# One written order of steps per engine for the first attention with the routing and shared expert beside it, without the identity matmuls before its scores

## The reference, cut to what matters

```
x = x + gated_recurrence_and_ffn(ln(x))           # layer 0, "front"
x = x + attention(ln(x), ctx, ctx)                # 16 heads of 8, rotary, key mask: the FIRST attention
x = x + mixture(ln(x))                            # shared expert + 8 routed experts, top 2, width 256
x = x + attention_of_24_picked_rows(ln(x))
x = x + attention(ln(x), ctx, ctx)                # the last attention
x = x + capacity_mixture(ln(x))                   # 8 experts of width 512

mixture(x):   probs = sigmoid(x @ router.T + bias); scores, idx = top_k(probs, 2); scores /= sum(scores)
              shared = (silu(x @ sg.T) * (x @ su.T)) @ sd.T
              routed = sum over the 2 experts e of a token: score_e * ((silu(x @ gate[e]) * (x @ up[e])) @ down[e])
```

## Time and profile before

| what | value |
|---|---|
| times of three runs | 775.45, 776.41 (median), 781.89 us |
| the profiled execution's own time | 780.67 us |
| its span, first to last instruction | 778.9 us (1.8 us around it) |
| mean granted PE clock | 0.878 of full speed |
| busy, share of the span | PE 77%, DVE 56%, PEld 56%, ACT 38%, POOL 30% |

### The profile page before, as it was taken

How to read it: one execution, slowest core, us unless ns; L and a number is a source line. 1 busy time by engine, 2 the same in 40 slices (tenths; PEclk the granted TensorE clock), 3 DMA queues, 4 the chain that set the end, 5 groups by cost and what they waited for, 6 DMA issues and landing times.

```text
span 778.9 us, 15307 instructions
## 1 busy us (share of the span) xinstructions
PE 601.5 (77%) x4751; PEld 432.5 (56%) x4751; DVE 438.5 (56%) x1165; ACT 296.2 (38%) x679; POOL 232.9 (30%) x324
## 2 busy tenths in 40 slices
PE   4699996898778849898716699846799987555992
PEld 2444453665555639798504488623466764534992
DVE  4889787566554554356334566355455642568443
ACT  2585320455334314343202277511145453101661
POOL 6735333001004545243621111022100001353452
PEclk9899998899996989999866899976799997657997
DMA  9955987543200083432100000108543500003014
GB/s 286 323 93 155 274 216 221 130 115 84 66 4 21 30 313 96 122 107 67 47 24 1 0 2 1 50 14 239 131 114 84 127 2 1 0 32 105 25 35 129
DMA packets 87492, 75.71 MB, mean 97 GB/s; under 512 B 10456, under 2 KB 80752, under 8 KB 84512
## 3 DMA queue, kind: packets, MB, share of 16 engines
q1 hardware_dynamic: 82544, 66.80, 31.7%
q0 software_dynamic: 3296, 6.79, 2.9%
q10 hardware_dynamic: 1584, 1.26, 0.5%
HBM read 41.59 MB, written 32.98 MB: 96 GB/s over the span
## 4 chain that ended last, share of the span: by engine, by line
PE 44%; DVE 20%; issue 11%; DMA 7%; POOL 6%; ACT 3%; SPq 3%; another core or an unknown queue 2%; DVEq 2%; POOLq 0%; ACTq 0%
PE ps L2220 5%; PE ps L2104 4%; PE ps L1782 3%; PE ps L1746 3%; PE ps L2088 2%; PE ps L2070 2%; SPq L426 2%; POOL xs_scr L779 2%; PE ps L2323 2%; PE ps L2232 2%; DMA q_scr<-parts 2%; PE ps L1930 2%; PE ps L2066 2%; PE ps L2083 2%
## 5 line engine op out<-in xcount | busy, mean ns | idle before, releaser
L1363 DVE TENSOR_REDUCE negm<-ps 128x4 f32<-128x512 f32 x128 | 85.1, 689 | 63.0 <-PE ps L2070 60.6
L955 ACT ACTIVATE wa<-ps 128x1024 f32<-128x1024 f32 x64 | 65.6, 1025 | 83.0 <-PE ps L2088 80.8
L2220 PE MATMUL ps<-nT,f 128*128 128x128 f32 x368 | 52.3, 287 | 11.3 <-DVE wb L1571 8.4
L2220 PEld LDWEIGHTS ps<-nT,f 128*128 128x128 f32 x368 | 47.1, 200 | 13.7 <-DVE wb L1571 10.0
L2104 PE MATMUL ps<-wa,f 128*32 128x128 f32 x1024 | 42.9, 294 | 2.9 <-ACT wa L955 1.9
L1854 PE MATMUL ps<-identb 128*128 128x512 bf16 x108 | 38.6, 418 | 4.8 <-issue 2.1
L2070 PE MATMUL ps<-stack 75*128 75x128 bf16 x384 | 40.6, 232 | 0.0
L2070 PEld LDWEIGHTS ps<-stack 75*128 75x128 bf16 x384 | 32.4, 105 | 14.6 <-issue 4.8
L711 POOL DMA_INDIRECT x_scr<-y_tok,selT x32 | 31.5, 985 | 28.0 <-ACT stack L1064 18.8
L2088 PE MATMUL ps<-stack 75*128 75x128 bf16 x384 | 35.5, 231 | 2.2 <-DMA stack<-mT 1.5
L784 POOL DMA_INDIRECT y_scr<-f,stack x23 | 25.8, 1121 | 31.5 <-DVE f L1721 21.1
(11 more groups left out here) (391 smaller groups left out, 1508.8 us busy)
## 6 DMA issues: line engine op xcount, KB each, us to landing
k_scr<-parts SPq DMA_DIRECT2D x48, 192.0 KB, 3.0
q_scr<-parts SPq DMA_DIRECT2D x48, 192.0 KB, 3.5
stack<-k_scr SPq DMA_DIRECT2D x12, 600.0 KB, 7.0
stack<-q_scr SPq DMA_DIRECT2D x12, 600.0 KB, 5.3
w_w<-in_w SPq DMA_DIRECT2D x2, 2048.0 KB
x_scr<-sel SPq DMA_DIRECT2D x2, 1472.0 KB, 10.3
x_scr<-stack SPq DMA_DIRECT2D x10, 256.0 KB, 4.9
wb<-q_scr SPq DMA_DIRECT2D x4, 600.0 KB, 5.0
```

Source lines behind the costliest of these rows:

```text
L955: link.release(act.activation(wa[:, u % 2, :], BF[u % 2], ACT.Exp, scale=SCALE), hWA.filled, hWA.at(stage, n * 4 + u), hB.freed)
L1363: v.tensor_reduce(negm[:, g4 * 4:g4 * 4 + 4, j], A[u % 2].rearrange("p (h k) -> p h k", h=4), AX.X, ALU.max, negate=True).then_inc(hA.free ...
L2220: last = mm(A[x % 2][:, c * S:(c + 1) * S], gu_of[x % NGU][:, c * S:(c + 1) * S], nT[:, k % 2, q * S:(q + 1) * S], start=True, stop=True)
```

## The change

The hooks go. Each engine gets one list (`WOVEN`) with every part of the eight steps and every mixture step in one order, "part unit . step" or "kind . block" (x is DVE's maxima, e ACT's exponentials, c POOL's copies, fa and fb the two sets of eight scatters of the first half). The last attention keeps its table, now `STEP`.

```diff
-    for op, u in STEP[0]: ... for s in extra(eng, n, op, u): mixture_step(s[:-2], int(s[-1]))
+    for s in WOVEN[eng]:  attention part, or mixture_step(s[:-2], int(s[-1]))

+        T_TURN = {s: k for k, s in enumerate(s for s in WOVEN["PE"] if s[0] in "MXo" and of_attention(s))}

         def mix_bank(step):
-            return U if step in ("tr.2", "ro.2", "bk.3", "ro.3", "cu.1") else T
+            return dict(T=T, U=U, Z=A[1])[bank_name(step)]
+        def bank_name(step):
+            return "Z" if step in ("po.2", "bk.2", "tr.2", "ro.2") else "U" if step in ("bk.3", "ro.3", "cu.1") else "T"

                 def maxima(n, u):
                     j, g4 = u // 4, u % 4
+                    if a == 0 and u == 0 and n > 0:
+                        v.wait_ge(mp_ready, n)
                     v.wait_ge(hA.filled, hA.at(stage, n * 8 + u))

+                    elif name == "Z":
+                        pe.wait_ge(hA.freed, hA.at("moe0", 1))

                 elif kind == "so":
+                    if n == 1:
+                        pe.wait_ge(dve_front, after("lg.2"))

-                    if a == 0 and True:
+                    if a == 0 and False:
                         keep_warm(bank, 1)

+            def first_rows(part):                       # POOL, fa.0 and fb.0
+                g.wait_ge(zero0_stored, 32)
+                g.wait_ge(dve_front, after("ps.0"))
+                for b in range(part * HB // 2, (part + 1) * HB // 2):
+                    scatter(b, 0)
```

More of the change, by code:

```diff
@@ L1438, in gu_copy @@
                  .then_inc(gu_ready, 1)
-            def closing(part):
-                for s in CLOSE["DVE"][part].split():
-                    mixture_step(s[:-2], int(s[-1]))
             def mixture_step(kind, n):
@@ L1985, in ring_T @@
                 T_next[0] = k + 1
-            def closing(part):
-                for s in CLOSE["PE"][part].split():
-                    mixture_step(s[:-2], int(s[-1]))
             def mixture_step(kind, n):
```

212 lines of the change are left out of this document (125 added, 87 removed), and 17 rows, old and new, of tables (BESIDE, CLOSE, STEP).

## The result

The changed kernel takes 776.33 us (median of 20 runs), the kernel before, timed beside it on the same chips, 781.82 us (20 runs): a ratio of 0.9928, 95% interval 0.9905 to 0.995. It is 5.5 us faster, 0.7%. The forecast said 24.4 us. Some executions of these kernels have a lower granted clock and a time 1 to 2.5% longer; the ratios leave them out.

The account below looks back on a forecast made before the run. No engine was full, PE nearest; the order in which engines wait for each other sets the time. Six steps -15.4, behind the attention -11.4, lost head start +2.4: -24.4 us, from 776.41 to 752.0, range 742 to 769.

Parts of the forecast that it names:

- the signs named: Marks of success: `M` of steps 1 and 7 some 67 us apart, DVE busy over 0.7, clock 0.8 or more.
- the lost head start: At the first routed product: two routed tiles no longer multiplied while DVE still places rows, +2.4 us.
- Part 1: Attention steps without the mixture: without eight identity matmuls (1.76 us of PE) a step takes 8.8 us instead of 10.5.
- Before 147.5: Ahead of the end of step 1's maxima: no gain counted, a load covers it; otherwise at most 3.5 us.
- Part 2: Attention steps with mixture work: the written order keeps DVE 0.88 busy, so the last three steps take 39.8 us.
- Part 3: From `M` of step 7 to the first routed product: DVE's 37 + 8 us plus 4.5 make 49.5 against 60.9.
- 4.5 for the clock: Behind the attention: 4.5 us added because PE idles long and its clock may fall, doubling about half its chained steps.
- POOL's chain as second limit at 44 us: Behind the attention: scatters, `rs.3` (waiting for `sb.3` at about 23) and load make the first tile ready at about 44 us.
- Small edits: Added `mp_ready` wait on DVE 0 to 0.3 us; bank `A[1]` for `po.2`, `so.1`'s wait and SP's order cost nothing.
- Rival (a): Only the matmuls' time returns: six steps lose 10.6 us, the part behind keeps 60.9; 8.2 us gained, 768; chance 0.16.
- Rival (b): Without identity matmuls PE's clock stays low from 147.5 on: 23 us slower, 800; chance 0.10.
- Rival (c): Steps 1 to 3 wait for their loads and stay at 10.5: 4.9 us lost, 757; chance within the forecast's 0.74.

Follow-up runs that it names:

- experiment 1: The changed kernel with the 64 identity matmuls put back ahead of the first attention's score groups: 775.06 us, ratio 0.9899 to the kernel before.
- Experiment 5: The changed kernel with sixteen plain stores for the first half's indirect scatters, rows left unsorted: 769.9 us, ratio 0.9877 to the kernel before.
- experiment 8: The changed kernel with POOL's first set of eight scatters waiting for the silu of block 0: 767.83 us, ratio 0.9847 to the kernel before.
- numbers 12: The kernel of 9 with plain stores in place of the first half's sixteen indirect scatters: 764.97 us, ratio 0.9835 to the kernel before.
- 14: The kernel of 9 with plain stores for scatters and PE's `tr.3` ahead of `so.1` and `so.2`: 763.25 us, ratio 0.9789 to the kernel before.
- experiment 2: The kernel before, in the old order, with only the identity matmuls taken out: 786.59 us, ratio 1.0024 to the kernel before.
- experiment 4: The changed kernel with POOL's `rs.3` ahead of all sixteen scatters of the first half: 777.2 us, ratio 0.9899 to the kernel before.
- 9: The changed kernel with the first scatters waiting for block 0's silu and `sg.0`, `su.0` moved later: 767.0 us, ratio 0.9814 to the kernel before.
- 3: The changed kernel with PE's `sg.0` moved behind `o0.7` and `su.0` behind `X1.7`: 775.36 us, ratio 0.9872 to the kernel before.
- 6: The changed kernel with half of the first attention's exponentials left out, output wrong: 768.97 us in one run.

## Why the prediction was wrong

**The sign was right, the size was not:** -4.2 us between the spans where -24.4 was forecast. (The 752.0 also starts from the median of three runs, 776.41; twenty runs have 781.82, so 5.4 us of the distance between 752.0 and 776.33 is the starting point, and the rest is the change.) Of the signs named, `M` of steps 1 and 7 are 77.1 us apart and not 67, DVE is busy for 0.60 of the time from 147.5 to the first product and not over 0.7, and the clock there is 0.87. By the forecast's own terms 5.1 us are missing ahead of `M` of step 7, 16.6 behind it, and the lost head start was 1.5 us cheaper (0.9 instead of 2.4; in the variants the time behind the first product lies between 483 and 489 us, so 0.9 can't be told from nothing). 5.1 + 16.6 - 1.5 = 20.2.

**Part 1, 8.8 us a step: failed, by 1.1 us a step.** Steps 2 to 4 take 10.1 us on average, where the forecast's three terms have 9.0. Two of its terms were too small. PE's busy time, 7.9 by the forecast, is 8.5 to 9.0: with the eight matmuls in, a step of the new order has 9.7 to 10.2 us of it, and not 9.66, and without them the two steps at the full clock have 1.3 and 1.6 less, and not 1.76 (experiment 1 against the changed kernel). And PE's waits, taken as 0.6 "as now", are 1.2 to 1.6. Put back, the eight cost a step 0.4 to 1.1 us; in the old order two steps gained 0.5 each without them. The closing loop was walked through PE and DVE only (and its pause of 1.1 us is less than its own 0.2 + 0.6 + 0.5). The rows of ACT show a third chain: three exponentials of 1.02 us, a store and a copy, 0.18 to 0.27 us apart, and PE waits for the copy's bank (156.77, 0.63 us). Half the exponentials gave 0.6 us a step, half the maxima 0.2; what makes up the rest of PE's waits is open. Over the three steps this is 30.3 us instead of 26.9: 3.4 us.

**Before 147.5, "nothing": right in the sum, wrong in the cover.** `M` of step 1 did come 5.3 us earlier, but step 2's first scores started at 148.27 (147.67 before). The cover that was named is the load. The load held them in experiment 1 (146.01, 1.23 us for the DMA). In the changed kernel they start 2.3 us later than there, with a clock of 0.51 instead of 0.92 ahead of them. Up to `M` of step 4, at 180.54, 33.0 us pass from 147.51 on where the forecast had 26.9. Of the 6.1, 3.4 are Part 1's, 0.6 the late start, and 2.1 are there because `M` now stands 2.0 us behind `A0` (178.58) where it stood 0.16 ahead of it.

**Part 2, the last three steps in 39.8 us: right in the number, by some luck.** From `M` of step 4 (180.54) to that of step 7 (219.30) 38.8 us pass (it was 48.2), although one of them lost time to the clock. With this 1.0 the 6.1 become the 5.1 above. But DVE is busy for 28.3 of the 38.8, where the forecast had 31.5 in 39.8: it had less work and stood for longer, and the two errors cancel. (With 0.05 us for each of the 93 gaps the 31.5 are 36.2, not 35.) The written order shortens the steps where DVE has mixture steps to fit in.

**Part 3, 49.5 us behind `M` of step 7: failed, by 16.6 us.** The step that failed is the walk of 37 + 8 us of DVE's work and waits. It took each engine's wait as the end of a chain over instructions, and gave POOL's scatters only POOL's time. `te.1` ends 64.1 us behind `M` of step 7, where the forecast had all of DVE's work and waits in 45 plus 4.5 for the clock. The runs show in its place:

- The scatters. Experiment 5 (plain stores) makes the part 58.3 us, 7.9 less. With them ACT waits 4.8 us too long at `K1.7` and DVE 2.3 us at `lg.3`, for signals of PE. The new order exposed this, because it brings the first set forward to 229.69, into the attention's last step; before, it began at 244.57, just behind ACT's last copy of the attention (244.09), so that this copy came 14.5 us behind `M` of step 7 where it now comes 22.1 behind it (17.4 without the hold, experiment 8). In the kernel before PE's signals came late beside the second set too (three of them, for matmuls that ended at 271.3 to 273.8, stand at 274.4 to 274.5), but no engine had to wait long for them.
- `sg.0` ahead of `V2.7`: 3.5 us of PE at the low clock on the attention's last chain. With plain stores in both, its later place, and the later first set, make the part 55.7 instead of 58.3: 2.6 us.
- `tr.3` behind two down projections: 0.6 us (numbers 12 and 14).
- Of the other 5.5 us, 2.1 stand between the end of `te.1` (283.17 + 0.18) and the first product (285.42): 1.74 without a releaser and a copy of weights. They are there before as well, 2.9 us, and the sum left them out. Another 1.28 is ACT's table load ahead of the silu (242.56), which stands before as well; no run took it away. The rest is not taken apart, and the cause of it stays open.

The clock did fall there, to 0.59 from 224 to 236.5 and 0.79 over the part; what that cost, no run separates from the rest, so the 4.5 us can't be called right or wrong.

**POOL's chain as second limit at 44 us** (its own terms give 39, with `rs.3` at 23) was late itself: `rs.3` stands at 255.3, 36 us behind `M` of step 7 and not 23, and the load of the sorted tiles is issued at 268.9, 49.6 behind it. But DVE was later still, and PE never waited for a tile ahead of the first product. It is right that POOL was looked at, but its price isn't a late tile.

**Small edits** show nothing that contradicts their zero. **Rival (a)** named a right reason (the chain behind the attention is the same in both orders) and came nearest: -8.2 us, against -5.5 by the medians. That is luck in part: its 10.6 us for the steps look like the 10.3 measured, but with the matmuls back `M` of step 7 comes as early (experiment 1), so the order brought them, and the part behind didn't keep its 60.9 us. **Rival (b)** is real in the old order, as experiment 2 shows (clock 0.74), with no change in the time beyond the interval; in the new order the clock fell in three stretches only (0.51 ahead of 147.5, 0.72 from 182 to 194, 0.59 from 224 to 236.5). **Rival (c)**, a step that waits for its load, is not seen in the changed kernel; waits of 0.3 to 1.2 us for a load stand ahead of one step's scores in the kernel before and in experiments 1 and 2. (Its 4.9 us are 4.6 by the forecast's terms, 3 x 10.5 against 26.9.)

**What is shown and what isn't.** Shown by taking away, moving and delaying the scatters (4, 5, 8, 9, 12): with them some of PE's signals come late, and ACT and DVE stand behind matmuls whose records have ended. Most of these waits end 0.5 to 0.7 us behind the last data of a set, in experiment 4 1.9 us behind it, and in experiments 3 and 6 within 0.2 us behind the data of one scatter in the middle of a set, so "until the set is down" isn't the rule. Number 12 adds that it isn't transfers from POOL as such, since with plain stores `lg.3` keeps its 0.04 us; but the last of these are down at 254.6, 3.5 us ahead of `lg.3`, so length and kind aren't fully told apart there either, only that no signal was late beside them. Not shown is by which way a scatter delays a signal of PE, and whether the matmuls themselves end late, since the ends in their records are modelled. No packets of the instruction queues lie in these waits.
